# GpSimd issues twelve of tile 0's routing scatters before tile 2's inverse deviation

## What is computed

```python
def _L0_ffn_ref(x, w_router, we1, we3, we2, ws1, ws3, ws2):   # x is layernorm(residual)
    probs = softmax(xt @ w_router)                            # 16 experts
    top_w, top_i = top_k(probs, 4); top_w /= sum(top_w)
    cw = zeros((T, E)).at[arange(T)[:, None], top_i].add(top_w)
    g = silu(einsum('td,edh->teh', xt, we1)) * einsum('td,edh->teh', xt, we3)
    moe_out = einsum('teh,ehd->td', g * cw[:, :, None], we2)
    shared = silu(xt @ ws1) * (xt @ ws3) @ ws2
    return shared / 5 + moe_out * 4 / 5
x = x + 0.5 * _L0_ffn_ref(layernorm(x), ...)
```

## Time and profile before

| what | us |
|---|---|
| median of three runs | 2915.84 |
| lowest and highest run | 2911.52, 2936.37 |
| the profiled execution, its device time | 2938.03 |
| its span, first to last instruction | 2935.9 |
| TensorE busy (share of the span) | 2516.6 (86%) |
| VectorE busy | 1944.9 (66%) |
| ScalarE busy | 1441.1 (49%) |
| GpSimd busy | 933.3 (32%) |

### The profile page before, as it was taken

The page is one execution under the profiler, slowest core; times in us unless marked ns, Lnnn a source line. Parts: engine busy times, 40 slices in busy tenths (PEclk is TensorE's granted clock), DMA queues, the critical chain, the costliest instruction groups (busy, mean ns, idle before and its releaser), DMA issues. The chain is left out here.

```text
span 2935.9 us, 51676 instructions
## 1 busy us (share of the span) xinstructions
PE 2516.6 (86%) x15894; PEld 1660.1 (57%) x15894; DVE 1944.9 (66%) x5584; ACT 1441.1 (49%) x3622; POOL 933.3 (32%) x1304
## 2 busy tenths in 40 slices
PE   6784988699899999958875888499788999998899
PEld 5663877556433333347765777388663333334787
DVE  5663666677688888746554666477468888875544
ACT  3331444333358778723332444234364878775443
POOL 3663555311322223315654555211022222221000
PEclk9886999899889999978877999699887999999899
DMA  5334444555634544353335444333254454543210
GB/s 153 136 135 116 146 145 146 163 192 205 173 71 88 115 97 98 101 170 130 136 114 142 145 146 145 141 125 119 70 165 107 95 110 89 111 106 109 82 37 29
DMA packets 256416, 359.82 MB, mean 123 GB/s; under 512 B 43493, under 2 KB 205590, under 8 KB 250006
## 3 DMA queue, kind: packets, MB, share of 16 engines
q1 hardware_dynamic: 220822, 249.53, 32.6%
q0 software_dynamic: 35328, 106.99, 9.7%
HBM read 199.16 MB, written 156.47 MB: 121 GB/s over the span
## 5 line engine op out<-in xcount | busy, mean ns | idle before, releaser
L1288 DVE CUSTOM_DVE_ANT_0 attn_heads_masked_s<-attn_heads_s_ps,attn_heads_causal 128x768 bf16<-128x768 f32 (+7 forms) x1024 | 726.7, 754 | 141.8 <-PE attn_heads_s_ps L1090 126.0
L1207 ACT ACTIVATE attn_heads_probs<-attn_heads_st_ps 128x512 f32<-128x512 f32 (+3 forms) x1536 | 663.6, 494 | 232.6 <-PE attn_heads_st_ps L1109 218.4
L2081 POOL DMA_INDIRECT y_dram<-moe_expert_y_sb,moe_expert_rows_y x288 | 276.2, 959 | 308.6 <-DVE moe_expert_y_sb L2210 128.8
L1125 PE MATMUL attn_heads_o_ps<-attn_heads_probs,attn_v_sb 128*32 128x512 f32 (+3 forms) x3072 | 329.1, 501 | 2.1 <-POOL attn_heads_probs L1032 1.9
L1602 POOL DMA_INDIRECT xs_dram<-moe_route_xn,rows_at x256 | 263.4, 1029 | 110.3 <-issue 77.1
L1032 POOL TENSOR_SCALAR_AFFINE_SELECT attn_heads_probs<-attn_heads_probs 128x512 f32<-128x512 f32 x256 | 163.2, 638 | 362.0 <-ACT attn_heads_probs L1207 356.8
L1109 PE MATMUL attn_heads_st_ps<-attn_heads_more_st 99*128 99x512 bf16 x960 | 261.7, 330 | 0.1
L1090 PE MATMUL attn_heads_s_ps<-attn_heads_more_st 96*128 96x512 bf16 (+1 forms) x960 | 247.2, 336 | 9.0 <-DVE attn_heads_row_max L1288 4.5
L2109 PE MATMUL moe_expert_gu_ps<-moe_w_hi,moe_expert_xT_hi 128*128 x576 | 191.7, 333 | 33.0 <-issue 23.9
L2151 ACT ACTIVATE moe_expert_xT_hi<-moe_expert_xT_ps 128x256 fp32r<-128x256 f32 x288 | 111.1, 386 | 215.3 <-PE moe_expert_xT_ps L2095 194.2
L1109 PEld LDWEIGHTS attn_heads_st_ps<-attn_heads_more_st 99*128 99x128 bf16 x960 | 84.5, 97 | 212.7 <-ACT attn_heads_probs L1207 159.4
(11 more groups left out here) (269 smaller groups left out, 6143.7 us busy)
## 6 DMA issues: line engine op xcount, KB each, us to landing
moe_expert_x_sb<-xs_dram SPq DMA_DIRECT2D x288, 136.0 KB
attn_stack<-y_dram POOLq DMA_DIRECT2D x32, 512.0 KB, 5.4
o_dram<-attn_heads_oT SPq DMA_DIRECT2D x64, 256.0 KB, 3.2
lut_y_sb<-y_dram POOLq DMA_DIRECT2D x32, 512.0 KB, 5.8
moe_route_w_raw<-in_L_ffn_we_dram SPq DMA_DIRECT2D x96, 128.0 KB
q_dram<-attn_proj_parts SPq DMA_DIRECT2D x32, 384.0 KB, 4.1
k_dram<-attn_proj_parts SPq DMA_DIRECT2D x32, 384.0 KB, 3.2
x_mid<-moe_route_x_sb SPq DMA_DIRECT2D x16, 512.0 KB, 4.5
```

Of the source, the lines that this page charges most:

```text
L1125: last = pe.matmul(o_ps[h * VW:(h + 1) * VW, use % OB, TILE - w:TILE], v_sb[:, at:at + VW], probs[:, G % NR, h, 0:w], start=(j == 0), stop ...
L1207: act.activation(probs[:, G % NR, h, 0:w], st_ps[:, v % NB, 0:w], ACT.Exp, scale=scale)\
L1288: dve.tensor_tensor_reduce(out=masked_s[:, use % 4, 0:w], in0=s_banks[:, at * TILE:at * TILE + w], in1=causal[:, SEQ - w:SEQ], scale=1.0, ...
L2081: pool.indirect_dma_start(y_dram, bass.IndirectOffsetOnAxis(rows_y[:, s % RI:s % RI + 1], 0), y_sb[:, s % AHEAD, :], None)\
```

## The change

Of tile 0's 16 scatters the first twelve (three groups) stand directly behind `rstd_of(1)`, then comes `rstd_of(2)`, then the last four. From tile 1 on the list is as before. It holds for both routing phases.

```diff
                 rstd_of(1)
-                for t in range(TILES):
+                scatter(0, range(SUB - 1))
+                rstd_of(2)
+                scatter(0, range(SUB - 1, SUB))
+                for t in range(1, TILES):
                     if t + 2 < TILES:
                         rstd_of(t + 2)
                     scatter(t, range(SUB))
```

## The result

The changed kernel took 2909.52 us (median of 22 runs, 2886.7 to 2932.32), the kernel before 2920.76 (22 runs, 2904.84 to 2947.09): a ratio of 0.9951, 95% interval 0.993 to 0.9973. It is faster by half a per cent, about 14 us by the ratio and 11 us by the medians, where 1.2 us more had been forecast. The time lies inside the forecast's range of 2903 to 2934 us; its direction does not fit the forecast.

A forecast was written before the change was run, and what follows sets the result against it. The VectorE and TensorE chain, not GpSimd, was taken to carry the routing phases, ending with `rows_at` of the last tile. Only the padding wait's 1.2 us was nonzero: 2915.84 + 1.2 = 2917.0 us, range 2903 to 2934.

The forecast's parts named there:

- no measurable change: Whole kernel: the main case, the time stays at 2917 us; chance 78%.
- Steps (1) and (2): GpSimd, both routing phases: twelve scatters start earlier, gain 0; tile 2's inverse deviation behind them is still in time, cost 0.
- rival of a late deviation: Tile 2's inverse deviation, both phases: the twelve scatters run too long and VectorE waits, 2920 us; chance 2%.
- Step (3): VectorE's padding wait, both phases: early scatters' DMAs delay it by 0.6 us each, 1.2 us together (0 to 2.2).
- third rival: VectorE's padding wait: padding packets let all twelve scatters by, 4.4 us per phase, 8.9 in all, 2925 us; chance 8%.
- Step (4): Tile 1's normalisation: scatters now run beside it, the scatter gives way, cost to VectorE 0.
- Gain on the path: 0, since nobody waits for them: GpSimd, both routing phases: moving twelve scatters forward saves nothing, as no engine waits for them.
- a slow stretch goes: First routing phase: breaking the scatter run ends TensorE's 0.70 us steps, 8.2 us less, 2908 us; chance 9%.
- the first rival: Both routing phases: GpSimd's backlog is on the path, so its lead gives back 33.7 us, 2882 us; chance 2%.

The follow-up runs named there:

- e5: The kernel before, unedited, profiled on a chip of the faster kind: 2710.01 us (one run).
- e6: The changed kernel, unedited, on a chip of the faster kind: 2707.32 us against 2709.71 for the kernel before, ratio 0.9996.
- e16: The kernel before with only the last four of tile 0's scatters moved behind tile 3's inverse deviation: 2965.76 us against 2959.17, ratio 1.0017.
- e8: The changed kernel with four of tile 1's scatters also ahead of tile 3's inverse deviation: 2906.41 us against 2924.53 for the kernel before, ratio 0.994.
- e9: The changed kernel with eight of tile 0's scatters issued again in GpSimd's pause: 2908.51 us against 2924.53 for the kernel before, ratio 0.9949.
- e15: The kernel of e8 again, on a slower chip: 2931.11 us against 2959.17 for the kernel before, ratio 0.9897.
- e18: The changed kernel, unedited, run again: 2911.57 us against 2928.47 for the kernel before, ratio 0.997 (0.9938 to 1.0002).
- e17: The kernel before with only four of tile 0's scatters ahead of tile 2's inverse deviation, twelve behind: 2921.36 us against 2928.47, ratio 1.0.

## Why the prediction was wrong

The forecast said "no measurable change", at 2917; measured was a gain of 14 us, a ratio of 0.9951, on the chip forecast for.

- **Steps (1) and (2), GpSimd's timing: right within 0.8 us.** Scatters started at 30.06, the deviation at 45.76 (forecast 46.6 to 47.7 for the end of the twelve), and the normalisation of tile 2 was unhindered. The rival of a late deviation has a slip: at 2 us a scatter it would have been 24.0 - 23.0 = 1 us late, not 2.
- **Step (3), 0.6 us per phase for the padding: about right in size, not shown as a cost.** The wait moved by +0.48 and -0.47 us. On the 2710 chip, e5 to e6, the time from the addresses to the end of the wait went from 5.59 to 4.96 us and from 5.07 to 5.26. The mean of the four is -0.1 us. The starved padding of the third rival did not happen. The prediction put the Trainium skill's rule (DMA: Bandwidth & Descriptors, section Queues, rings and completion order), by which a completion count lands only after the earlier writes of its DMA engine, across queues, at the upper end of the term, 1.1 us in a phase. None of these four waits grew by more than half a microsecond.
- **Step (4), VectorE beside scatters: right in its cost, loose in its reading.** Tile 1's normalisation, which now has scatters beside it, took 1.37 us in both phases (1.38 before, with GpSimd idle). The changed kernel's rows:

```profile
35.42 0.96 POOL L1602 DMA_INDIRECT xs_dram<-moe_route_xn,rows_at  x1 [0.30 <-issue]
35.44 1.37 DVE L1797 TENSOR_SCALAR moe_route_xn<-moe_route_x_sb,moe_route_moments,moe_route_rstd 128x256 f32<-128x256 f32 x4
```

The scatter of 1.85 us at 56.06 in the kernel before was not the normalisation's doing alone: that one ended at 56.22, and VectorE's next operation (line 1958) ran from 56.13 to 57.08. The scatter at 54.62, which did run beside the normalisation, took 1.13 us.
- **The step that failed** is the term "Gain on the path: 0, since nobody waits for them" of (1), drawn from "Whatever GpSimd gains in tile 0 is therefore lost in these gaps, and the end of the phase is set by `rows_at` of the last tile". Both halves of that sentence are right on this chip; what was wrong is to conclude a gain of 0. In the profiled executions the two routing phases gave 19.3 and 10.9 us, in the runs the whole gave about 14. I asked only who waits for a scatter's result, found nobody, and took the length of each tile as given. But the addresses came 20.9 us sooner, because the tiles of 30 to 39 us that make those gaps got shorter when scatters were moved. The term should have had a far end: three stretches of 84.1 us could fall towards three of the shortest of them, 3 x 22.7 = 68 us in each phase. They fell to 67.9 in the profiled execution, in one more profile of the change to 68.8 and 84.3.
- **The rival that came nearest** is "a slow stretch goes" (9%, 8.2 us). It named the right place, the 0.70 us steps behind a long run of scatters, and took one tile of one phase for its price; that tile alone fell by 14.6 us (38.64 to 24.05). The argument "no wait names the scatters" was weak: the waits for late updates in the rows above end in "remote" or "issue" and name no engine. Its guess that breaking the run is the cause is refuted by e16, where a break of 9 us brought nothing.
- **On a 2710 chip the forecast holds:** 0.9996 (0.9984 to 1.0008) against +1.2 us. There tiles are not slowed, and the first rival, the lead that reaches the end, is true in part: 2.2 us of 17.

What is shown: the change is faster on the chip forecast for, and its variants e8, e9 and e15 are clear of noise on two 2920 chips, while its one repeat there (e18) is not. On the 2710 chips it gains nothing that can be measured. In the profiles the gain comes with fewer slow tiles in the routing phases, on chips where TensorE's updates come late while scatters run. It does not need a pause of 16 us (e9), it does not follow from a break alone (e16), and it is not VectorE waiting less for deviations: on the 2920 chip it waited only for tile 0's, in both kernels.

What is not shown is the cause. That the number of scatters beside the products brings it is supported by the stretches and by the order of e16, e17 and e18; the intervals of e17 and e18 overlap, and e9 fits it badly. That GpSimd's queue position brings it (Q) fits e9, e16, e17 and e18 within their intervals and was not tested by itself. A kernel with few scatters in the first two stretches and the queue position of before would part the two. It stays open too what makes the updates late, and whether the recording of the trace has a part in the 0.70 us steps. Timed runs differ between the chips as the profiled ones do, but they don't tell that.

## What to carry to other kernels

When an engine's instructions are moved, ask not only who waits for their results but what runs beside them in the old place and in the new: work that nobody waits for may still go with a slower pace of the engine that bounds, as here. Idle time put down to "issue" or "remote" on a bound engine, and tiles of equal work that take 22.8 and 38.6 us, are a stock of time that a harmless reordering may free, and belong in the range. And a gain of half a per cent measured on one chip may be a property of that chip: run both kernels on a second one before building on it.

## What the runs showed of the hardware

The two kinds of chip differ almost only in the phases with scatters: of the 228 us between the spans of these two profiles, about 223 lie in the two routing and the two expert phases. From the kernel before, the routing phase from its first addresses to the experts, the expert phase, and the attention heads, first on the 2920 chip and then on the 2710 chip:

```profile
29.92:289.01 259.09, 183.31 (x1024) 154.82 (x1024) 141.79 (x480) 74.86 (x114) 139.36 (x140) 0.80 0.41 130
289.01:560.47 271.46, 242.20 (x1728) 209.85 (x1728) 172.89 (x575) 126.21 (x576) 135.57 (x142) 0.99 0.45 143
793.50:1279.75 486.25, 472.22 (x3281) 178.27 (x3282) 399.07 (x1106) 348.13 (x806) 141.99 (x220) 0.96 0.46 100
```

```profile
29.79:234.54 204.75, 158.10 (x1023) 139.47 (x1023) 141.06 (x480) 75.15 (x114) 140.82 (x140) 0.88 0.53 165
234.54:451.49 216.95, 214.53 (x1727) 205.72 (x1728) 176.22 (x575) 132.94 (x576) 135.98 (x142) 0.99 0.57 179
681.96:1169.76 487.80, 473.17 (x3282) 179.16 (x3282) 399.11 (x1106) 348.07 (x806) 141.75 (x220) 0.96 0.45 100
```

The attention heads, without a scatter, take the same (486.25 and 487.80 us); the expert phase, with 144 scatters, takes 271.46 against 216.95 at the same clock share of 0.99, and routing 259.09 against 204.75. A scatter takes GpSimd the same time on both (median 0.96 us). TensorE's updates are up to about 11 us late in the routing phases of the one (mean 2 to 3) and about 0.6 us in the mean of its expert phases; on the other they are at most 0.02 us late in all of routing, and 0.04 us in the mean of the expert phases. What sets the two kinds of chip apart is not shown.
